# Moving the row-weight sums of a bias term from PSUM to SBUF, and two of them to another place in VectorE's order

## The reference

```python
hidden = concatenate([cond_512, cond_512], axis=-1)          # (4, 512)
x_mean = mean(x, axis=1, keepdims=True)                      # x: (4, 1024, 512)
fused = concatenate([x, x_mean * ones_L, hidden[:, None, :] * ones_L], axis=-1)
out = x + relu(einsum('bld,do->blo', fused, W) + b)          # W: (1536, 512)
```

## Time and profile before

| | |
|---|---|
| median of 3 runs | 103.94 us (103.73 to 104.02) |
| profiled execution, whole time | 103.58 us |
| its span in the trace | 101.8 us, so 1.8 us lie around it |
| PE busy | 97.3 us, 96% of the span |
| DVE busy | 83.8 us, 82% |
| ACT busy | 48.2 us, 47% |
| POOL busy | 38.9 us, 38% |
| bytes moved | 21.41 MB, mean 210 GB/s |
| granted clock of TensorE | 1.00 |

### The profile page before, as it was taken

One profiled execution on the slowest core, in us unless ns is written; L12 is line 12 of the kernel. 1 busy time (PEld: TensorE's weight loads), 2 busy tenths in 40 slices (PEclk: granted clock), 3 DMA queues, 4 the chain that ended last, 5 costly groups with the idle time before them and its releaser, 6 DMA issues.

```text
span 101.8 us, 1678 instructions
## 1 busy us (share of the span) xinstructions
PE 97.3 (96%) x523; PEld 78.5 (77%) x523; DVE 83.8 (82%) x161; ACT 48.2 (47%) x118; POOL 38.9 (38%) x35
## 2 busy tenths in 40 slices
PE   5999999999999999999999998999999989999990
PEld 2359999888888788688888885888888858888890
DVE  3165679899899999999999989999998999585671
ACT  3267335966506549879649300964844007300000
POOL 1039600000000000799885504578577529930000
PEclk9999999999999999999999999999999999999999
DMA  1999986999999999999999800591590690699973
GB/s 58 286 294 262 258 200 171 268 238 219 260 332 261 247 243 240 243 243 249 292 356 344 257 2 6 107 266 38 129 265 18 151 251 21 183 245 251 262 284 115
DMA packets 35504, 21.41 MB, mean 210 GB/s; under 512 B 2084, under 2 KB 33192, under 8 KB 35496
## 3 DMA queue, kind: packets, MB, share of 16 engines
q1 hardware_dynamic: 34424, 20.40, 80.8%
q10 hardware_dynamic: 1072, 0.92, 3.1%
HBM read 12.91 MB, written 8.39 MB: 209 GB/s over the span
## 4 chain that ended last, share of the span: by engine, by line
PE 46%; DVE 36%; ACT 8%; issue 6%; DVEq 0%
PE ps_y L504 29%; DVE ps_xt L356 8%; DVE back L369 7%; DVE xl L362 6%; DVE ps_const L390 6%; PE ps_mean L501 6%; ACT xh L279 5%; PE ps_y L624 4%; PE ps_y L622 4%; PE ps_y L623 4%; DVE ps_const L385 3%; DVE w2x L390 2%; DVE bsum L382 2%; ACT relu_t L299 1%; ACT relu_t L286 1%
## 5 line engine op out<-in xcount | busy, mean ns | idle before, releaser
L251 POOL TENSOR_TENSOR xa<-xa,back 128x512 f32 (+1 forms) x26 | 33.5, 1310 | 44.7 <-DVE back L369 44.7
L504 PE MATMUL ps_y<-xh,w1h 128*128 128x512 f32 (+1 forms) x128 | 43.6, 367 | 0.0
L504 PE MATMUL ps_y<-xl,w1h 128*128 128x512 f32 (+1 forms) x128 | 43.0, 363 | 0.0
L504 PE MATMUL ps_y<-xh,w1l 128*128 128x512 f32 (+1 forms) x128 | 42.9, 363 | 0.0
L279 ACT ACTIVATE xh<-ps_xt 128x512 fp32r<-128x512 f32 (+1 forms) x36 | 19.7, 550 | 18.1 <-DVE ps_xt L356 18.0
L504 PEld LDWEIGHTS ps_y<-xh,w1h 128*128 128x128 f32 x128 | 22.6, 188 | 4.9 <-issue 1.2
L356 DVE STREAM_TRANSPOSE ps_xt<-xa 128x512 f32<-128x512 f32 (+1 forms) x36 | 22.3, 642 | 4.9 <-DMA xa<-in_x_dram 4.6
L504 PEld LDWEIGHTS ps_y<-xh,w1l 128*128 128x128 f32 x128 | 22.6, 189 | 3.8
L504 PEld LDWEIGHTS ps_y<-xl,w1h 128*128 128x128 f32 x128 | 22.7, 189 | 3.6
L362 DVE TENSOR_TENSOR xl<-ps_xt,xh 128x512 fp32r<-128x512 f32 (+1 forms) x36 | 22.2, 620 | 3.1 <-ACT xh L279 3.1
L299 ACT ACTIVATE relu_t<-ps_y,bias 128x512 f32<-128x512 f32 x18 | 12.3, 688 | 16.2 <-DVE bias L407 12.7
(11 more groups left out here) (40 smaller groups left out, 45.0 us busy)
## 6 DMA issues: line engine op xcount, KB each, us to landing
xa<-in_x_dram SPq DMA_DIRECT2D x62, 128.0 KB, 4.1
out_dram<-xa SPq DMA_DIRECT2D x28, 256.0 KB, 4.1
w<-in_L_cond_W_dram SPq DMA_DIRECT2D x4, 256.0 KB, 4.7
w<-in_L_cond_W_dram SPq DMA_DIRECT2D x2, 512.0 KB, 6.0
w<-in_x_dram SPq DMA_DIRECT2D x4, 256.0 KB, 5.0
out_dram<-w SPq DMA_DIRECT2D x3, 256.0 KB, 4.0
w<-in_L_cond_W_dram SPq DMA_DIRECT2D x8, 64.0 KB, 3.1
w<-in_L_cond_W_dram ACTq DMA_DIRECT2D x8, 64.0 KB, 3.6
```

Of the source, the lines that this page charges most:

```text
L251: nc.gpsimd.tensor_tensor(rows, rows, back[:, t], ALU.add).then_inc(added, 1)
L504: return nc.tensor.matmul(ps_y[:, t, ls], lhs, rhs, start=start, stop=stop, skip_group_check=True)
```

## The change

The three partial sums and the final one all stand in `w2x` (SBUF); `ps_const` is left to `const_product`, which no longer waits for the sums. The four one-column additions of `bsum` become one addition of four columns. Batch 3's `mean_terms` moves from behind `turn_back(20)` to ahead of `turn_back(19)`, where batch 2's stands for `turn_back(11)`. (`w2x_step` counts as before; `bsum_ready` counts batches instead of columns.)

```diff
-        ps_const = psum("ps_const", [P, D])
+        ps_const = psum("ps_const", [P, NL])
...
-                for k in range(NK):
-                    nc.vector.tensor_scalar(bsum[:, k:k + 1], xsum[:, H * b + 1, k:k + 1], xsum[:, H * b + 2, k:k + 1], None,
-                                            ALU.add).then_inc(bsum_ready, 1)
-                dve.wait_ge(bsum_ready, NK * b + 1)
-                nc.vector.tensor_scalar(ps_const[:], w2[:, 0], bsum[:, 0:1], None, ALU.mult).then_inc(w2x_step, 1)
+                nc.vector.tensor_tensor(bsum[:], xsum[:, H * b + 1], xsum[:, H * b + 2], ALU.add).then_inc(bsum_ready, 1)
+                dve.wait_ge(bsum_ready, b + 1)
+                nc.vector.tensor_scalar(w2x[:], w2[:, 0], bsum[:, 0:1], None, ALU.mult).then_inc(w2x_step, 1)
                 for k in range(1, NK):
-                    dve.wait_ge(bsum_ready, NK * b + k + 1)
                     dve.wait_ge(w2x_step, NK * b + k)
-                    sums = w2x if k == NK - 1 else ps_const
-                    nc.vector.scalar_tensor_tensor(out=sums[:], in0=w2[:, k], scalar=bsum[:, k:k + 1], in1=ps_const[:],
+                    nc.vector.scalar_tensor_tensor(out=w2x[:], in0=w2[:, k], scalar=bsum[:, k:k + 1], in1=w2x[:],
                                                    op0=ALU.mult, op1=ALU.add).then_inc(w2x_step, 1)
...
-                if n == NK * (H + 1) - 1:
+                sums = n in (NK * (H + 1) - 1, NK * (2 * H + 1) - 1)
+                if sums:
 
                     x_low(n_x)
                     n_x += 1
-                    mean_terms(2)
+                    mean_terms(n // NK // H + 1)
                 turn_back(n)
...
-                if n == NK * (H + 1) - 1:
+                if sums:
                     continue
-                if n == NK * (2 * H + 1):
-                    mean_terms(B - 1)
...
                 pe.wait_ge(cond_spread, 1)
-
-                pe.wait_ge(w2x_step, NK)
                 pe.wait_ge(w3_landed, 16 * 2)
```

## The result

The changed kernel takes 105.62 us (median of 6 runs) against 103.85 for the kernel before in the same measurement: a ratio of 1.0172, with a 95% interval from 1.0137 to 1.0207. It is 1.8 us slower. The forecast was 104.35 with a range from 103.4 to 105.0, so the direction was right and the size outside the range. The profiled execution took 105.42 us, with a span of 103.6.

A forecast was written before the change was run, and what follows sets the result against it. PE, busy 97.3 of 101.8 us, was taken as the bound, with a nearly full DMA. Stores delayed by the move let the DMA end the span at 102.15, +0.4: 103.94 + 0.4 = 104.35 us, range 103.4 to 105.0.

The forecast's parts named there:

- PE's two waits: PE idles ahead of mean_bias(2) and mean_bias(3), about 0.42 and 0.44 us; both go, together worth 0.86 us.
- The move's effect on the stores: turn_back(19) behind the sums delays POOL's add 19, so SP issues group 4's stores 4.3 us later, from 83.1.
- the signs that were named: No PE idle at mean_bias, mean_terms 3.2 us, late stores, DMA share over 0.95, no SP wait before its last store.
- mean_terms: One batch's sums on DVE: 3.24 us instead of 3.77, bounds 3.15 to 3.60, saving 0.5 us a batch.
- The collision with POOL: Sums reading two SBUF tiles could lose up to one POOL add, 1.3 us, once; priced at nothing, POOL being idle.
- rival A: At the tail the DMA sets the end: span +0.1 to +1.1 us, point +0.4; chance 0.55.
- last_bias issued: In SP's queue, the bias line lands behind group 4's data, so last_bias goes out at 88.5, at worst 89.2.
- DMA full: The DMA is full 0.86 us after group 5's first store is issued at 88.9, so at 89.75.
- full for: DMA work left: 8.2 us for groups 5 and 6, 3.1 for group 7's rows, 0.3 for last_bias; 11.6 together.
- from there to the end of the span: From the DMA being done, at 101.35, to the span's end: 0.8 us, as in the kernel before.
- Rival D: Sums gain nothing from SBUF (3.6 us) and the bias line lands late, at 89.2: span 1.2 us longer, 105.1; chance 0.09.
- Rival E: Multiplication and sums collide with POOL: w2x 1.3 us later, stores 1.3 later still, +1.7 us, 105.6; chance 0.03.

The follow-up runs named there:

- sbuf_in_place: Changed kernel with batch 3's sums in SBUF but back at their old place behind turn_back(20); 0.9988 of the kernel before.
- after_again: The changed kernel run once more, unaltered, beside the repeat of the run with only delayed stores; 1.0186 of the kernel before.
- line_first: Changed kernel with the bias line's four small DMAs issued ahead of group 4's stores; 1.0117 of the kernel before.
- late_stores: Changed kernel with turn_back(19) ahead of the last x_low again, and SP awaiting the fourth bias before group 4's stores; 1.0132 and 1.0105 of the kernel before.
- no_store4: Changed kernel without group 4's four stores, the last wait counting four less; 1.0015 of the kernel before.
- psum_moved: Kernel before with only the move of batch 3's sums ahead of turn_back(19), sums still in PSUM; 1.0260 of the kernel before.
- line_on_act: Changed kernel with the bias line's four small DMAs in ACT's queue instead of SP's; 1.0029 of the kernel before.
- psum_turn19: Kernel before with batch 3's sums moved ahead of turn_back(20) only, all sums still in PSUM; 0.9992 of the kernel before.

## Why the prediction was wrong, point by point

**Right.** PE's two waits are gone. Their worth was put at 0.86 us, and PE ended 0.7 us earlier, in a profile in which it was 0.17 us later at `const_product` (33.45 against 33.28 for the last matmul ahead of it). The move's effect on the stores was followed link by link: stores of group 4 at 83.05, measured 82.99; bias line at 86.1, measured 86.08. Of the signs that were named, the DMA share from 90 to 101 is 0.95; one failed, as SP still waits 0.9 us for DVE before its last store (1.6 before).

`mean_terms` was put at 3.24 us, with 3.15 as the lower bound, and takes 3.04 (77.85 to 80.89): the multiplication at 0.50 measured 0.49, the multiply-adds at 0.72 measured 0.75, but the waits were put at 0.1 each and are 0.04 or less. So 0.73 us is saved on batch 3 and not 0.2 to 0.6. The Trainium skill, "VectorE: DVE Perf Modes", section "The perf-mode tier table", gave 0.27 us less for the fp32 `tensor_scalar`; the rows show 0.746 - 0.486 = 0.26, and agree.

The collision with POOL was priced at nothing here, and there was none. Where it does occur (`sbuf_in_place`), the page "SBUF — State Buffer" of the Trainium skill, section "Who interferes with whom", read as in the prediction, would have the first multiply-add wait until the add ends, 1.1 us from 78.80 to 79.91. Measured were 0.9 us, so the rule holds nearly. The add was itself 0.24 us longer; as it began at 78.38, while the multiplication (78.27 to 78.76) was running, the profile doesn't tell which of the two lengthened it.

**Wrong in size.** The step that failed is rival A's sum, "89.75 + 11.6 = 101.35" and the 0.8 us behind it: the stretch from group 5's first store to the end of the span. It was put at 102.15 - 88.9 = 13.25 us. Measured were 103.6 - 89.61 = 13.99, and 14.57 in the second profile of the changed kernel (`after_again`). The kernel before could have warned: there it is 101.8 - 87.14 = 14.66. Term by term, from the bias line on:

| term | put at | measured | second profile |
|---|---|---|---|
| last_bias issued | 88.5 (88.1 to 89.2) | 89.22 | 88.54 |
| group 5's stores issued | 88.9 | 89.61 | 88.93 |
| DMA full | 89.75 | 91.0 | 90.0 |
| full for | 11.6 | 11.0 | 11.0 |
| from there to the end of the span | 0.8 | 1.6 | 2.5 |
| end of the span | 102.15 | 103.6 | 103.5 |

The term that failed in both profiles is the last one. The 0.8 us is right from the last bytes moved to the end of the span (101.0 to 101.8 before, about 102.8 to 103.6 after). But the sum puts it right behind the full stretch, and so puts at nothing, without a reason, the time in which a full DMA runs out: 0.8 us here, 1.2 in `line_first`, 1.8 in the second profile.

The other two differ between the profiles. The line behind the stores took 0.7 us more than the point in the first, just beyond the bound, with 1.71 us for issuing the four where the forecast kept 1.12; in the second it was on the point, and the miss was as large. From group 5's first store to a full DMA it took 1.4 and 1.1 instead of 0.86. In the kernel before, the share was already 0.50 when that store was issued (87.0 to 87.5); in the changed kernel it was 0.00 (89.5 to 90.0). This is a likely reason, and no run tests it. The 0.6 us of full stretch went the other way, as part of the work is done while the DMA fills and runs out. Together 1.25 - 0.6 + 0.8 = 1.45 us, which is the miss in the span.

**The chances.** The place where the slowdown comes from, the late stores and a full DMA, had 0.55 + 0.09, and that was right. Rival D's span, 1.2 us longer, was nearer than A's 0.4 (measured 1.8), but half of its reason, that the sums gain nothing, was wrong. Rival E's 105.6 is the measured time by luck: its collision didn't occur. The range of A ended at + 1.1, since none of its terms held the run-out.

**Shown and open.** That the late stores cost the time is shown by adding them (`late_stores`), by leaving them out (`no_store4`) and by the move alone (`psum_moved`). That the bias line behind them is a good part of it is shown by `line_on_act` and `line_first`. That POOL's row of adds takes the gain is argued from `no_store4` and `psum_turn19`. What the changed kernel pays beyond `late_stores` (0.4 to 0.8 us) is open, and so is why a full DMA takes 0.8 us to run out in one profile and 1.8 in another.

## What to carry to other kernels

When a step is moved ahead of a small one, ask what the small one releases at the end of its chain, and in which queue that stands. Here one 0.7 us transpose held back 1 MB of stores by 4.2 us, and behind them a dependent round trip through memory. Put work that only prepares (sums, biases) behind the step that frees a store, and that step into a hole where the engine waits anyway. And when a transfer system comes near to being full until the end, count its last store from a full queue: here 3.1 to 3.9 us to land instead of 1.7. Check the sum against the same stretch of the kernel before: a forecast of 13.25 us for what took 14.66 needs a reason.

## What the hardware showed that I had not expected

- A `scalar_tensor_tensor` of 128x512 fp32 with a column of scalars takes 0.752 us from SBUF and 0.754 with PSUM as input and output. So the memory makes no difference for it. The one with a constant takes 0.693; that the column makes this difference isn't shown, as that one also has other operations (max and add).
- Beside a POOL add, one multiply-add with two tiles in SBUF took 1.67 us instead of 0.75 (`sbuf_in_place`).
- Four stores of 0.5 KB behind 1 MB of stores took 3.1 us from the first issue to SP going on (2.8 in the second profile), against 2.0 with no stores ahead of them (`no_store4`); from ACT's queue they took 4.5 from the first issue (2.3 of it the issuing), while the same 1 MB moved.
- After a full stretch the DMA share doesn't fall at once. The last bytes move 0.8 to 1.8 us behind its end, and the last 128 KB land after 3.1 us (3.9 in `line_first`), against 1.7 in the kernel before.
